# A fused attention and expert block on one core: the order of each engine's work, taken from step counts before and from a list scheduler on a modelled clock after

## The reference, cut to what matters

```
for i in range(16):                               # heads, in order
    q_rot, k_rot = rotary(q[:, i]), rotary(k[:, i])
    att = q_rot @ k_rot.T * scale
    if i: att = att + cascade_w[i - 1] * cascade_bias
    att = softmax(where(causal, -inf, att))
    out_i = att @ v[:, i]
    cascade_bias = mean(att, axis=1)              # column means bias the next head
x = layernorm(x + concat(out) @ Wproj)
sel, rw = argmax(x @ gate.T), sigmoid(max(x @ gate.T))
x = layernorm(x + expert[sel](x * rw))            # u * silu(g) @ w_down.T, 256 -> 128 -> 256
```

## Time and profile before

| | us |
|---|---|
| median of 3 runs | 3635.12 |
| lowest, highest | 3629.88, 3637.76 |
| the profiled execution, its own time | 3630.31 |
| its span, first to last instruction | 3628.5 |
| mean granted TensorE clock | 0.968 |

### The profile page before, as it was taken

One profiled execution on the slowest core, in us unless ns is written; L12 is line 12 of the kernel. 1 busy time (PEld: TensorE's weight loads), 2 busy tenths in 40 slices (PEclk: granted clock), 3 DMA queues, 4 the chain that ended last, 5 costly groups with the idle time before them and its releaser, 6 DMA issues. The chain is left out here.

```text
span 3628.5 us, 92399 instructions
## 1 busy us (share of the span) xinstructions
PE 3125.4 (86%) x29690; PEld 1588.7 (44%) x29690; DVE 2593.1 (71%) x7831; ACT 3115.0 (86%) x8936; POOL 2015.4 (56%) x6194
## 2 busy tenths in 40 slices
PE   5788888888998889988998898898988888889865
PEld 3333333333444434444444443444444444344654
DVE  7566666666777776877877778687777767777664
ACT  3899999999998988988888899889878899999544
POOL 5555555554555366775665555666666533445356
PEclk8899999999999999999999999999999999999988
DMA  4332323334333434444443433345434333345465
GB/s 158 97 71 64 79 59 69 84 64 95 96 82 88 111 84 109 116 117 112 122 112 97 108 77 80 97 122 140 118 94 102 91 89 73 77 101 140 129 197 165
DMA packets 222518, 370.64 MB, mean 102 GB/s; under 512 B 49941, under 2 KB 165405, under 8 KB 209936
## 3 DMA queue, kind: packets, MB, share of 16 engines
q1 hardware_dynamic: 205968, 323.19, 35.9%
q0 software_dynamic: 14976, 37.34, 3.8%
q10 hardware_dynamic: 1088, 4.19, 0.3%
HBM read 259.76 MB, written 104.40 MB: 100 GB/s over the span
## 5 line engine op out<-in xcount | busy, mean ns | idle before, releaser
L1135 DVE CUSTOM_DVE_ANT_0 att_a<-scores,window 128x128 f32<-128x128 f32 (+7 forms) x2048 | 1509.0, 755 | 804.2 <-PE scores L808 650.7
L993 ACT ACTIVATE att_a<-att_a,neg_max 128x128 f32<-128x128 f32 (+7 forms) x2048 | 1597.8, 780 | 116.7 <-DVE neg_max L1135 113.3
L1005 ACT ACTIVATE att_t<-scores 128x1024 f32<-128x1024 f32 (+7 forms) x2048 | 1334.4, 652 | 175.5 <-PE scores L827 165.3
L825 PE MATMUL scores<-q_stack,k_stack 104*128 104x512 bf16 (+3 forms) x3072 | 819.3, 334 | 333.8 <-ACT att_t L1005 140.5
L843 PE MATMUL pv<-att_t,v_sb 128*32 128x256 f32 (+7 forms) x16384 | 828.5, 297 | 7.4 <-DVE o_sb L1169 6.9
L808 PE MATMUL scores<-k_stack,q_stack 99*128 99x512 bf16 (+3 forms) x3072 | 735.0, 334 | 27.3 <-DVE neg_max L1135 10.1
L1470 POOL TENSOR_SCALAR guess<-row_sum 128x8 f32<-128x8 int32 x256 | 55.0, 215 | 1138.8 <-ACT att_a L993 1137.9
L843 PEld LDWEIGHTS pv<-att_t,v_sb 128*32 128x32 f32 x16384 | 376.2, 109 | 513.1 <-issue 427.1
L825 PEld LDWEIGHTS scores<-q_stack,k_stack 104*128 104x128 bf16 x3072 | 240.0, 98 | 739.3 <-DVE neg_max L1135 363.3
L827 PE MATMUL scores<-identb,mask 128*128 128x128 bf16 x2048 | 455.6, 222 | 0.0
L1005 ACT ACTIVATION_READ_ACCUMULATOR att_t<-scores 128x1 f32 x2048 | 427.3, 209 | 0.0
(11 more groups left out here) (359 smaller groups left out, 4199.2 us busy)
## 6 DMA issues: line engine op xcount, KB each, us to landing
runner_r<-in_experts SPq DMA_DIRECT2D x137, 384.0 KB, 3.7
qk_parts<-of_proj SPq DMA_DIRECT2D x128, 384.0 KB, 2.8
q_stack<-qk_parts SPq DMA_DIRECT2D x378, 128.0 KB
k_stack<-qk_parts SPq DMA_DIRECT2D x378, 128.0 KB
of_proj<-in_xt SPq DMA_DIRECT2D x28, 1024.0 KB, 5.4
head_out<-o_sb SPq DMA_DIRECT2D x252, 64.0 KB
x_rows<-finisher_f SPq DMA_DIRECT2D x26, 514.0 KB, 4.7
finisher_f<-head_out SPq DMA_DIRECT2D x52, 256.0 KB, 5.0
```

The lines of the kernel that those rows point to most:

```text
L825: engine.matmul(scores[:, c0:c1], ks[0:ROWS_B, j * P:(j + 1) * P], qs[0:ROWS_B, j * P + c0 - base:j * P + c1 - base], start=True, stop=True)
L993: engine.activation(taken, taken, EXP, scale=-1.0, bias=neg_max[:, n, i:i + 1], accum_out=row_sum[:, n, i:i + 1]).then_inc(s_exp_a, 1)
L1005: engine.activation(att_t[:, ring:ring + end - base], scores[:, base:end], EXP, accum_out=col_sum[:, n, j:j + 1]).then_inc(s_exp_b, 1)
L1135: engine.tensor_tensor_reduce(out=att_a[:, ring:ring + end - base], in0=scores[:, base:end], in1=window[:, T - (end - base):T], op0=ALU.ad ...
```

## The change

The first projections keep their order. Everything behind them is ordered anew. The tables `FILL_ORDER`, `TAKE_ORDER`, `VALUE_ORDER`, `PE_PLACES`, the gaps and phases are gone. `timetable()` now returns one list for each engine, made by a simulation of the kernel on a modelled clock:

- ACT's 4096 exponentials and the `egl`s keep their fixed sequence (`main`). The other engines have queues of attention work: on PE `fill_a`, `fill_b`, `pv` and `rows`, on DVE `take`, `rows_copy`, `o_move`, on POOL `guess`, `parts`, `lack`, on SP `rows_out`.
- Every operation has a modelled cost (`work`, `SIDE`, `ON_SCALAR`), every transfer an issue time and a landing on one shared DMA line (`moved`). `needs` lists what it waits for, `due` when it must be done for ACT's sequence to go on.
- `choose` takes on each engine, at each moment, the attention operation whose needs are done, the earliest due first, or a side stage that can start before it. A side stage must pass `fits`: with it in front, the next two operations of each queue must not become later than they are, beyond `TOLERANCE`. A stage that has waited `OVERDUE` (8 us, or 2 us where it holds a bank) goes in without that. On ACT `fits` isn't asked.
- `bank_for` refuses a bank that would be missing when `rows` is ready.
- Jobs begin at the same units as before (`turn`), but all 12 `stack` loads of a head and the four `hout` stores are jobs of their own (rank -1, first among side work) that begin at a unit's start, where before they stood one in each step.

The operations themselves stay as they are, with small exceptions: `qk_sin` is split into `qk_cross` and `qk_sin` on POOL, `f_add` into `f_add` and `f_stat` on DVE, `f_norm` into four stages, and one routing operation into two, so that other work may go between them. The multi-instruction POOL step at the start of a unit becomes three stages, `guess`, `parts` and `lack`.

```diff
-    PE_PLACES = (1,2,0,1,0,1,1,2)
+    HANDOVER = 0.035
+    LANDING = 2.0
+    BANDWIDTH = 220e3
+    OVERDUE = 8.0
+    TOLERANCE = 0.05
+    MARGIN = 1.0
+    HOLDING = 2.0
...
+    SIDE = dict(
+        qk_a=("PE", 0.87), qk_b=("PE", 0.87), qk_turn=("DVE", 1.24), qk_cross=("POOL", 1.42), qk_sin=("POOL", 1.36),
...
+        t_scale=("DVE", 0.28), t_turn=("PE", 0.44), t_turned=("DVE", 0.34), t_gu=("PE", 0.88), t_tanh=("ACT", 0.16),
...
+            if kind == "fill_a":
+                busy = cols_a(key[1]) * 0.42e-3 + 0.01
+                return busy, busy + 0.165
+            if kind == "fill_b":
+                busy = cols_b(key[1]) * 0.42e-3 + 0.07
+                return busy, busy + 0.165
+            if kind == "pv":
+                busy = cols_b(key[1]) * 0.42e-3 + 0.2
+                return busy, busy + 0.07
+            if kind == "take":
+                busy = cols_a(key[1]) * 1.0417e-3 + 0.078
+                return busy, busy + 0.082
+            if kind == "exp_a":
+                busy = cols_a(key[1]) * 0.8333e-3 + 0.279
+                return busy, busy + 0.1
+            if kind == "exp_b":
+                busy = cols_b(key[1]) * 0.8333e-3 + 0.143
+                return busy, busy + 0.1
...
+        def due(kind, key):
...
+            elif kind == "fill_b":
+                t = start_of(("exp_b", key)) - HANDOVER
...
+            elif kind == "rows_out":
+                t = due("fill_b", (key - 1, 0)) - 0.8 - LANDING - 0.3
...
+        def fits(engine, t, busy):
+
+            after = lateness(engine, t + busy)
+            before = lateness(engine, t)
+            return all(a <= max(b, 0.0) + TOLERANCE for a, b in zip(after, before))
...
+                if engine != "ACT" and not anyhow and t - since[id(job)] < (HOLDING if holds(s) else OVERDUE) and not fits(engine, t, side_time(s)):
+                    continue
...
+        def moved(kind, t, busy):
+            size = MOVES[kind][2]
+            dma_free[0] = max(dma_free[0], t + busy) + size / BANDWIDTH
+            return dma_free[0] + LANDING
...
+            if slot == 2 and hh + 1 < GROUPS * NH:
+                loads = 2 * PRODUCTS + (SLOTS if (hh + 1) % NH == 0 else 0)
+                begin([Stage("stack", (hh + 1, n)) for n in range(loads)], -1)
...
-            for st in steps:
-                x_, i = st.x, st.i
-                if x_ is not None:
-                    for n, (which, block) in enumerate(FILL_ORDER[i]):
-                        if which == "a" and x_ < UNITS:
-                            fill_a(x_, block)
...
+            for stage in orders["PE"]:
                     kind, n = stage.kind, stage.key
                     room = bank_ap(stage.bank) if stage.bank is not None else None
-                    if kind in ("qk_a", "qk_b"):
+                    if kind == "fill_a":
+                        fill_a(*n)
+                    elif kind == "fill_b":
+                        fill_b(*n)
+                    elif kind == "pv":
+                        att_v(*n)
```

More of the change, by code:

```diff
@@ new lines, in timetable, with commit_side @@
+        rows_bank = {}
+        def commit_side(engine, t, job, b):
+            s = job.pop(0)
+            busy = side_busy(s)
+            if s.hold:
+                s.bank = b
+                s.before = used_by.get(b)
+                bank_until[b] = float("inf")
+                bank_end[b] = t + s.hold
+                held_by[id(job)] = b
+            elif s.frees or s.kind in MIDWAY:
+                s.bank = held_by[id(job)]
+            put(engine, s, 2 if over[0] else 1)
+            engine_free[engine] = t + busy
+            if s.kind in MOVES:
+                done[s.kind, s.key] = moved(s.kind, t, busy)
+                since[id(job)] = t + busy
+            else:
+                finish = t + busy + (0.165 if engine == "PE" else 0.1)
+                done[s.kind, s.key] = finish
+                since[id(job)] = finish
+            if s.frees:
+                used_by[s.bank] = (s.kind, s.key)
+                bank_until[s.bank] = done[s.kind, s.key]
+            if not job:
+                active.remove(job)
@@ new lines, in project, with onward @@
+            begin([x_stage(m)], 0)
+        def onward():
+            for g in range(GROUPS - 1):
+                if ("finish", g) in waiting and not any(waiting["finish", g]) and not any(waiting.get(("tiles", g - 1), [])):
+                    del waiting["finish", g]
+                    waiting["route", g] = [begin(route_job(g), 1)]
+                if ("route", g) in waiting and not any(waiting["route", g]):
+                    del waiting["route", g]
+                    waiting["tiles", g] = [begin(job, 2 + g) for job in tile_jobs(g)]
@@ new lines, in after_attention @@
+        def after_attention():
+            over[0] = True
+            g = GROUPS - 1
+            ended = max(engine_free["ACT"], engine_free["DVE"])
+            for b in range(2, 7):
+                bank_until[b] = ended
+                used_by[b] = ("attention", 0)
+            begin(route_job(g), 0)
+            for r_ in range(RUN[g]):
+                ahead = list(range(r_, TILES, RUN[g - 1])) if r_ < RUN[g - 1] else []
+                begin([Stage("t_weights", (g, r_), after=(("r_op", (g, ROUTE_OPS - 1)),) + tuple(
+                    ("t_stat", (g - 1, j)) for j in ahead[-1:]))], 1)
+            for job in tile_jobs(g):
+                begin(job, 2 + g)
@@ L1529, in pool_program @@
+            crossed_at = {}
+            for stage in orders["POOL"]:
+                    kind, n = stage.kind, stage.key
+                    if kind == "guess":
+                        guess_of(n)
+                    elif kind == "parts":
+                        parts_of(n)
+                    elif kind == "lack":
+                        lack_of(n)
+                    elif kind == "qk_cross" or kind == "qk_sin" and stage.era == 0:
                         cols = slice(n % 2 * WB, (n % 2 + 1) * WB)
```

1124 lines of the change are left out of this document (686 added, 438 removed).

## The result

| | median (runs) | profiled execution | span | units 0 to 63 | units 64 to 255 | end part |
|---|---|---|---|---|---|---|
| before | 3632.65 (4) | 3630.31 | 3628.5 | 772.2 | 2522.3 | 242.5 |
| after | 3493.34 (4) | 3503.37 | 3501.6 | 772.6 | 2439.9 | 194.9 |

All in us. The ratio of the times is 0.9618 [0.9598, 0.9637]: 139 us faster in the medians, 127 us between the two profiled executions. A second pair of profiled runs of the same two kernels gave 775.1 / 2517.1 / 242.3 before and 764.3 / 2442.1 / 189.0 after, so a stretch repeats within some 8 us. One of the eight executions of before in that second measurement took 6637 us where the other seven took 3626 to 3647, and it is left out. The windows of before are those of the earlier trace rows.

The account below looks back on a forecast made before the run. PE and ACT, with equal work, bound units 64 to 255 at 89% each, losing the rest waiting for each other. Gains 109 + 10 + 25 = 144 us from 3630.3 give 3486, 3490 as median; forecast 3488 us, 8-in-10 range 3380 to 3630.

Parts of the forecast that it names:

- B: Whole kernel: ACT's idle falls to 2.5% throughout, attention gains 236 us and the end 35, time 3364 us; chance 0.12.
- D: Whole kernel: the clock sorts what doesn't bind, the order comes out much as before, no change; chance 0.05.
- Units 64 to 255: Attention beside side work: at 5.5% idle PE needs 2413 us, a gain of 109 us, bounds nothing and 184.
- Rival A: Units 64 to 255: PE's 89% is its ceiling, a gain of 3 us there, time 3607 us; chance 0.19.
- Units 0 to 63: First stretch: ACT's 11.7 us wait for the value projection goes; gain 10 us, bounds 0 and 25.
- The row chain: Row transfer: issued at once instead of 5.3 us after lack in the example; part of the 109 us.
- Rival C: Stack-load bursts delay the row transfer, 3.5 us a head, 220 us, time 3711; PE waits every fourth unit; chance 0.14.
- The end part: After attention: left-over tiles' scatters (17 us) and PE work (8) go, gain 25 us; bounds loss of 10, gain of 50.
- POOL, DVE, SP: Other engines: split stages cost nothing on POOL and DVE (DVE 79% at 2413 us); SP's effect counted within the row term.

Follow-up runs that it names:

- e4: Changed kernel with OVERDUE and HOLDING both 0, so side stages never yield to what ACT needs soon: 3749.93 us, ratio 1.0107 to the kernel before.
- e1: Changed kernel with t_tanh counted ready 1.5 us later by the scheduler: 3554.14 us on a slow chip, ratio 0.9591 to the kernel before.
- e8: Changed kernel with tiles of groups 0 and 1 let in one every 1.5 units: 3477.06 us, ratio 0.9557 to the kernel before.
- e10: As e9, with t_tanh also counted ready 1.5 us later, as in e1: 3444.96 us, ratio 0.9462 to the kernel before.
- e3: Changed kernel with group 2's finishers begun 20 units later, leaving 8 tiles to the end part: 3551.11 us on a slow chip, ratio 0.9572 to the kernel before.
- c_after: The changed kernel, unchanged, measured again on another chip: 3490.46 us, ratio 0.9622 to the kernel before.
- e7: Changed kernel with group 2's finishers begun 27 units later, so 54 tiles run in the end part: 3511.43 us, ratio 0.9644 to the kernel before.
- e2: Changed kernel with a head's 12 stack loads each tied to a pass-A exponential over two units: 3576.89 us on a slow chip, ratio 0.9643 to the kernel before.
- e9: As e8, with the stack loads also spaced as in e2: 3458.48 us, ratio 0.951 to the kernel before.
- e5: Changed kernel with OVERDUE 20 us instead of 8: 3508.58 us, ratio 0.9658 to the kernel before.

## Why the prediction was right, and where it was off

The forecast was 3488 us, the changed kernel took 3493: the terms were off by more than their sum, so the closeness is luck. The range and the mechanism held: attention took 3212.5 us (the forecast set 3230 as its limit), and its part of the gain, 82 us, is the larger. Rivals B (ACT above 97%; it is at 91.5%) and D (no change) are out.

*Units 64 to 255: forecast 109 us, measured 82.* The mechanism is as forecast. ACT's two waits were to fall to about 150 us and fell to 140.9; e4, with 234.9, shows that the due times do it. Bare work came out as worked out (PE 2271 for 2280, ACT 2234 for 2252). The step that failed is the idle share: "With the idle share of the first stretch (5.5%)" gave PE 94.5%, and it reached 93.1%, ACT 91.5%. I had said that PE at 94% would stand against it and taken the figure all the same. My list of waits had no name for the tile's turn between PE and ACT, 51.7 us at the tanh, because the steps had kept it short. e1 shows that taking this wait away alone gains nothing; e8 to e10 show that tiles apart (15 to 17 us), then spaced loads (2) and then a later tanh (12.6) bring the stretch to 2410.5 us, about what I had forecast (2413). What else keeps the idle share up is open. Even there ACT is idle for 7.6% and PE busy for 93.8%, so the 5.5% was too low in any order tried. Rival A, that PE's 89% was a ceiling, is out.

*Units 0 to 63: forecast 10 us, measured 0* (8 to 11 in the second run and in e3). Six profiles with the same lists there (after, c_after, e1, e3, e7, e8) took 763 to 774 us, the two of before 772 and 775, so the gain lies between nothing and 12. The wait at `v_move` (11.7 us) is gone, as said. "What can be late next is the transfer itself" was the right question, priced at nothing here: PE's wait for `q_stack`<-`rowsT` rose from 1.3 us in 2 places to 17.6 in 14, with PE's clock lower besides (last section). e2 and e9, with the loads spaced, took 746 us: 26 us better than before, just beyond my upper bound of 25. ACT's longest wait of the stretch, 13.2 us (8.1 before), is not from the burst: e2 and e9 have it too (12.8 and 13.0).

*The row chain.* "The clock sends it at once" came true in part. In the unit of e2's excerpt lack is done at 214.55 (L1902, 214.35 + 0.20) and the transfer is issued at 215.73, 1.2 us later, where the earlier trace rows have 5.3. But both are single units, and that of the earlier trace rows was one of the slow ones. The median of this step over units 64 to 255 fell from 2.8 to 2.1 us, and the units above 3 us from 76 to 30; in units 0 to 63 it stayed (2.35 and 2.31). Little was won there, and the transfer took it back: 45.1 us of waits in 30 places before (43.8 + 1.3), 41.2 in 37 after. Rival C was real in kind. I priced it at 3.5 us a head for 63 heads, 220 us; the dearest wait is 2.5 us, and the whole is 41. Its condition (from 2.3 us a head) was not met: 41.2/63 = 0.65. Its sign, a wait in every fourth unit, did show: in units 0 to 63, 13 of the 14 waits stand some 48 us apart, which is four units (one place between them is empty).

*The end part: forecast 25 us, measured 48.* The 25 were for the left-over tiles alone, and those gave 26 to 32 (e7). The step that failed is "the order there was by a clock already", from which I took no gain: with the new list the same 54 tiles took 21 us less. Which of its costs or rules does that, and how much of it is e7's higher clock there, was not tried.

*POOL, DVE, SP: nothing,* and nothing showed: DVE is at 79% in units 64 to 255 (1937.7/2439.9), as worked out.

The start of attention lies 2.7 us later (94.2 for 91.5). So the 127 us of the profiled executions are 82 + 48 - 3, against 109 + 25 + 10 = 144. Two errors of some 25 us cancelled, by luck, and the first stretch's 10 was lost to the burst.

## What to carry to other kernels

When two engines with equal work bound a stretch, price a better order by the busy share that the fuller engine will then have, and don't borrow the idle share of a stretch in which that engine had room. Look then for the next hand-over between the two (here the tanh between two matmul groups), and test it by moving it: where removing it gains nothing, the other engine may simply be late, and spreading its side work is the next thing to try. A scheduler that knows its engines but not its DMA queues will bunch loads ahead of a small transfer that someone waits for; give such loads places of their own.

## What was not expected of the hardware

A row transfer reached PE 4.9 us after its issue behind ten stack loads and four stores. My estimate from the Trainium skill, "DMA: Bandwidth & Descriptors", section "Anatomy of one DMA", had twelve such loads moved in 3.6 us; that section fits transfers issued by GpSimd, and these are issued by SP. The trace shows them take longer. SP issues the ten from 206.34 to 214.88 (4.9 us of its time, 0.33 to 0.60 each, the rest stores and a wait), and from 212 to 217 the DMA engines are full at 175 GB/s, so loads are still under way when the transfer comes.

TensorE's mean granted clock in units 0 to 63 follows the waits for that transfer: 0.96 and 0.97 where PE stood 17.6, 16.7, 13.4 and 13.8 us for it (after, e5, c_after, e8), 0.99 where it stood 1.3 us or only a few times (before, e2, e9). The trace of after shows the falls one by one. From 120 us to the end of that stretch the clock goes from 2.4 to 1.2 GHz nine times, for 44.5 us in all. Each of the nine begins during one of the 14 waits or within 2.3 us of its end, and of the ten waits of 1 us or more only one passes without. (In c_after it is five falls of six.) In before, e2 and e9 there is no fall in that stretch after 120 us. Windows of PE in after, then one matmul of the same shape at either level, then the window of e9:

```profile
120.00:866.80 746.80, 667.83 (x6462) 0.97 0.30 72
219.70:226.50 6.80, 5.87 (x29) 0.50 0.17 56
...
363.05 0.31 PE L1228 MATMUL scores<-identb,mask 128*128 128x128 bf16 x1
367.03 0.22 PE L1228 MATMUL scores<-identb,mask 128*128 128x128 bf16 x1
...
120.00:838.40 718.40, 649.26 (x6442) 1.00 0.33 75
```

With the same work PE is busy 683, 685, 676 and 674 us against 666 in e2 and e9. So the burst's 16 to 31 us (763 to 777 for 746) have two parts, the waits and the slower matmuls behind them. Each is of some 8 to 19 us, and together they are more than the difference (17.6 + 17 for 26.5 in after), since other waits shrink beside them. No run keeps the waits and holds the clock up, so that the first brings the second rests on where the falls stand.

One chip ran the kernel before in 3714 us where the other three measurements gave 3629 to 3638, yet the new kernels' attention there was as long as elsewhere (units 0 to 191 of e3 2421 us, of after 2424 and of c_after 2414).
